# An attention block with gated experts on one core: own order for the last unit, V copied ahead, a wider low pass, another opening

## The chip, the cores and the metric

One core of a Trainium2 chip runs the whole computation. It has TensorE (PE; its weight loads are listed as PEld), VectorE (DVE), ScalarE (ACT), GpSimd (POOL) and SyncE (SP), which issues the DMAs. The metric is the device time in microseconds of one execution; lower is better.

## The reference

For x of 8 x 256 x 512 (2048 tokens), in float32:

```
xn = layernorm(x)
q, k, v = xn @ wq.T, xn @ wk.T, xn @ wv.T      # 32 query heads, 8 key/value heads, 128 wide
q, k = rotary(q), rotary(k)                    # q*cos + rotate_half(q)*sin
s = q @ k.T / sqrt(128), scaled for some keys, causal mask; p = softmax(s)
s_out = (p @ v) @ wo.T                         # each key head serves 4 query heads
gates = softmax over the top 2 of 4 router logits of xn
g = silu(sum_e gates_e * (xn @ A_e.T) @ B_e.T) # experts of rank 16
out = x + s_out * g
```

## The kernel before

**Precision.** Every large matmul runs in a reduced float form (fp32r), in three passes: each operand is split into a high part (a rounded copy, made by ACT) and a low part (the rest, made by DVE; for weights both parts by POOL), and hi*hi, hi*lo and lo*hi are added in PSUM (`three_pass`).

**Units.** The work is cut into 32 units: 8 key heads (groups) times 4 blocks of 512 tokens. A unit has four items: 2 sequences times 2 pairs of query heads. While unit u does its attention, PE also projects the keys, queries and V of later units. 16 tiles of 128 tokens gather the output in `y_sum`, one part for each of the 8 groups.

**One unit on PE** (`pe_unit`): for each item it transposes the probabilities (`turn_probs`, L565), computes the scores of the item two further on (`scores`, L554 to L558, into `pair`), multiplies probabilities with V (`prob_value`, L574, into `pv_ps`) and, between these, projects (`project`, L487, into `bank_a` or `bank_b`) or multiplies a tile with the output weights (`output_heads`, L581). Unit u finishes the last two output tiles of unit u-1. The transposes of item j wait for its scaled probabilities (`probs_ready`), the scores of item j+2 wait for both parts of item j's transposed probabilities (`pT_ready`), since they share a PSUM pair, and a product with V waits until the previous one has been taken from `pv_ps` (`attn_ready`).

**ACT and DVE** run lists in the same fixed order (`act_unit`, `dve_unit`). For an item: ACT copies the low scores (`low_scores`, L837), DVE masks and takes row extremes (`mask_rows`, L1215 to L1224), ACT takes exponents (L852), DVE inverts the sums (L1234), ACT scales (`normalise_rows`, L863), PE transposes, ACT makes the high part (`rows_high`, L871), DVE the low one (`rows_low`, L1204). The attention result is split by `attn_high` (L878) and `attn_low` (L1199). For a projected query head ACT swaps halves (`swap_halves`, L802 and L803), DVE multiplies by cos (L1169), POOL by sin (L391), DVE adds (L1178), ACT and DVE split (L810, L1184). V is copied by ACT (`copy_vT`, L824), transposed by PE (L544) and split. The next key projection into `bank_a` waits for the copy (`vT_done`).

**The experts** are side steps woven into units 0 to 7 (`side_plan`). The last of them, `d`, 16 times, multiplies the gated ranks `gm_T` (high part in partitions 0 to 63, low part in 64 to 127) first with `b_hi` on 128 partitions (L533), then the upper 64 partitions with `b_lo` (L534). The result becomes silu and goes to DRAM.

**The opening** is written out by hand (`pool_opening`, `act_opening`, `dve_opening`): statistics (L1047 to L1059), normalising shift of tiles (`x_shifted`, L945), transposes of x (`turn_x`, L494), their split (`x_high` L756, `x_low` L1073), the first weights (`first_high` L950, `first_low` L382). PE runs small matmuls (`keep_clock`, L705) until x is there.

**The end.** In the last group each tile gets its last part (`add_tile`, L1244), is multiplied with the gate (L1249) and gets x added by POOL (`add_residual`, L397). x and gate are loaded two tiles ahead by SP (`load_xg`). The last two tiles are computed in `pair[0]` after unit 31, each as two heads, then two more; DVE does all three operations on them (L1244, L1249, L1253) and SP stores them (`store_tile`).

Of the kernel before, what the change touches and what calls it, by code (L numbers as in the profile page):

```python
# [13 lines left out]
P = 128  # L14
# [47 lines left out]
def build(nc, x, w_seq, a_r, b_t, tables, out):  # L62
# [5 lines left out]
    with ctx:  # L68
# [36 lines left out]
        b_lo_full = sb("b_lo", [P, DM], F32R)  # L105
        b_lo = b_lo_full[0:ER, :]
# [54 lines left out]
        xg = [(mid_flat[:, 0:DM], mid_flat[:, DM:2 * DM]), (raw[:, 0, :], raw[:, 1, :]), (rot[:, 0, :], cosx[:, 0, :])]  # L161
# [66 lines left out]
        xg_in = [sem(f"xg_in{i}") for i in range(3)]  # L228
        y_gated = sem("y_gated")
        y_final = sem("y_final")  # L230
# [59 lines left out]
        def _(sp):  # L290
# [67 lines left out]
        def _(pool):  # L358
# [39 lines left out]

            def group(g, g_next):
# [3 lines left out]
                for i in range(first, BLOCKS):  # L403
# [38 lines left out]
                    if g_next is None:  # L442
                        add_residual(4 * i, 0)
                        if i < 3:
                            add_residual(4 * i + 1, 1)

            def pool_opening():
# [15 lines left out]
                sin_product(H2, 1)  # L463
                sin_product(H3, 1)
                sin_product(K, 2)
                inverse_std(3)
                sin_product(H0, 2)
                sin_product(H1, 2)
                split(0, WO)
                sin_product(H2, 2)  # L470
                split(0, WO + 1)
                split(0, WO + 2)
                sin_product(H3, 2)
                split(0, WO + 3)
# [7 lines left out]
            add_residual(TILES - 3, 1)  # L482
# [14 lines left out]
        def pe_side(u, j, p):  # L497
# [33 lines left out]
            else:  # L531
                t = i % BLOCK_TILES
                nc.tensor.matmul(o_ps[:, :], gm_T[:, t * P:(t + 1) * P], b_hi[:, :], start=True, stop=False)  # L533
                nc.tensor.matmul(o_ps[:, :], gm_T[0:ER, t * P:(t + 1) * P], b_lo, start=False, stop=True)\  # L534
# [163 lines left out]

        @block.tensor
        def _(pe):  # L700
# [44 lines left out]
            pe_unit(LAST)  # L745
            n = 4 * UNITS

            for t in range(2):
                output_heads(1, t, pair[0][:, t, :], range(0, 2))
            pe.wait_ge(attn_ready, n)  # L750
            for t in range(2):
                output_heads(1, t, pair[0][:, t, :], range(2, GROUP)).then_inc(o_done, 1)
# [128 lines left out]
        def act_unit(u):  # L881
# [70 lines left out]
        def act_opening():  # L952

            x_shifted(0, 1, 1)
            x_shifted(1, 2, 2)
            x_shifted(2, 3, 3)
            x_shifted(3, 4, 4)
            first_high(WK)
            first_high(WQ)
            x_high(0, first_banks[0])  # L960
            x_high(1, first_banks[1])
            x_high(2, first_banks[2])
            first_high(WQ + 1)
# [6 lines left out]
            x_shifted(4, 8, 5)  # L970
            q_high(H0, 1, None)
            swap_halves(H1, pv_ps, 1, H0, 1)
            swap_halves(H2, o_ps, 1, K, 1)
            x_high(4, first_banks[4])
            x_high(5, first_banks[5])
            k_high(1, None)
# [3 lines left out]
            q_high(H2, 1, None)  # L980
            q_high(H1, 1, None)
            swap_halves(H3, FIRST_H3, 1, H1, 1)
            first_low_scores()
            x_shifted(8, 12, 6)
            q_high(H3, 1, None)
            exponents(0, 1)
            v_high(1, None, pv_ps)
            normalise_rows(0, 1)
            swap_halves(H0, bank_b, 2, H3, 1)
# [12 lines left out]
            exponents(2, 3)  # L1002
            act_side(0, 1, 1)
            low_scores(3, 4)
            k_high(2, 4)
            q_high(H1, 2, 3)
            normalise_rows(2, 3)
            act_side(0, 1, 2)
            swap_halves(H2, bank_b, 2, K, 2)
            copy_vT(2, 1)  # L1010
            attn_high(1, 2, None)
            act_side(0, 1, 3)
            rows_high(2, 3, 2)
            exponents(3, 4)
            act_side(0, 2, 0)
            swap_halves(H3, bank_b, 2, H1, 2)
            act_side(0, 2, 1)
            attn_high(2, 3, None)
            low_scores(0, 5)
            normalise_rows(3, 4)  # L1020
            q_high(H2, 2, 4)
            swap_halves(K, bank_a, 3, H2, 2)
            q_high(H3, 2, 4)
            swap_halves(H0, bank_b, 3, H3, 2)
            rows_high(3, 4, 3)
            exponents(0, 5)
# [4 lines left out]
            exponents(1, 6)  # L1031

        @block.scalar
        def _(act):
            nc.scalar.dma_start(ident, tables[:, T_IDENT:T_COLS]).then_inc(ident_in, 16)

            act_opening()
            for u in range(1, WRITTEN):
                act_unit(u)
            loop(act, WRITTEN, LAST - 1, act_unit)  # L1040
            act_unit(LAST - 1)
            act_unit(LAST)
# [41 lines left out]
        def split_b():  # L1084
            nc.vector.wait_ge(bhi_done, 1)
            nc.vector.tensor_tensor(b_lo, b_raw[0:ER, :], b_hi[0:ER, :].bitcast(F32), ALU.subtract)\
                .then_inc(blo_done, 1)
# [148 lines left out]
        def add_tile(tile, done, start=False, final=None, bank=None, xg_set=None, tail=False):  # L1236
# [13 lines left out]
            if tail:  # L1250
                dve.wait_ge(y_gated, final + 1)
                dve.wait_ge(y_final, final)
                nc.vector.tensor_tensor(y, y, xg[xg_set][0], ALU.add).then_inc(y_final, 1)  # L1253
# [78 lines left out]
        def dve_opening():  # L1332

            first_statistics(0)
            first_statistics(1)
            first_statistics(2)
            shifts(0, 1, 1)
# [9 lines left out]
            block_statistics(2)  # L1347
            shifts(4, 8, 5)
            cos_product(K, bank_a, 1)
            cos_product(H0, bank_b, 1)  # L1350
            rotate(H0, 1)
            rotate(K, 1)
            q_low(H0, 1)
            cos_product(H1, pv_ps, 1, H0, 1)
            cos_product(H2, o_ps, 1)
            x_low(4, first_banks[4])
            x_low(5, first_banks[5])
            k_low(1)
            rotate(H2, 1)
            rotate(H1, 1)  # L1360
            x_low(6, first_banks[6])
            x_low(7, first_banks[7])
            q_low(H1, 1)
            q_low(H2, 1)
            shifts(8, 12, 6)
            cos_product(H3, FIRST_H3, 1, H1, 1)
            rotate(H3, 1)
            mask_rows(0, 1)
            q_low(H3, 1)
            row_inverse(1)  # L1370
            block_statistics(3)
            mask_rows(1, 2)
            rows_low(0, 1)
            v_low(1, pv_ps)
            cos_product(K, bank_a, 2, H2, 1)
            row_inverse(2)
            cos_product(H0, bank_b, 2, H3, 1)
            rotate(H0, 2)
            rotate(K, 2)
            attn_low(0, 1)  # L1380
            shifts(12, 16, 7)
            q_low(H0, 2)
            rows_low(1, 2)
            mask_rows(2, 3)
# [4 lines left out]
            dve_side(0, 1, 1)  # L1389
            mask_rows(3, 4)  # L1390
            k_low(2)
            q_low(H1, 2)
            dve_side(0, 1, 2)
            cos_product(H2, bank_b, 2)
            dve_side(0, 1, 3)
            attn_low(1, 2)
            rows_low(2, 3)
            rotate(H2, 2)
            dve_side(0, 2, 0)
            row_inverse(4)  # L1400
            cos_product(H3, bank_b, 2, H1, 2)
# [20 lines left out]
        def _(dve):  # L1422
# [4 lines left out]
            for u in range(FINAL, UNITS):  # L1427
                dve_unit(u)
# [44 lines left out]
```

## Time and profile before

| | before |
|---|---|
| runs, us | 1341.77, 1343.22, 1343.50; median 1343.22 |
| profiled execution, us | 1342.1 |
| its span, us | 1340.3 |
| PE busy | 1317.3 us, 98% |
| PE weight loads | 1106.4 us, 83% |
| DVE busy | 957.8 us, 71% |
| ACT busy | 971.7 us, 72% |
| POOL busy | 419.9 us, 31% |
| mean granted clock of PE | 0.994 |
| HBM over the span | 32 GB/s |

Busy shares are means over the whole span. A matmul's listed duration includes the filling and draining of the array and overlaps its neighbours: the distance between two starts says what it costs. The granted clock of a stretch is the mean of two levels, full (2.4 GHz) and half (1.2 GHz).

### The profile page before, as it was taken

What the parts mean: (1) busy time and instruction counts of PE and PEld (TensorE: products, weight loads), DVE (VectorE), ACT (ScalarE), POOL (GpSimd) and SP (SyncE); (2) the same over time, 40 slices, a digit from 0 to 9 for tenths busy, and PEclk for the clock granted to TensorE, in tenths of its full rate; (3) what the DMA queues carried; (4) which work ended last, traced back from release to release, by engine and by line L of the source; (5) the groups of instructions that cost most, each with busy time, mean ns of one, the idle gap of its engine ahead of it and who ended that gap; (6) DMA issues with size and microseconds to landing.
All of it is one profiled execution on the core that took longest, in us unless ns stands there. A gap on an engine that the chain in (4) does not pass through costs nothing.

```text
span 1340.3 us, 22644 instructions
## 1 busy us (share of the span) xinstructions
PE 1317.3 (98%) x7000; PEld 1106.4 (83%) x7000; DVE 957.8 (71%) x2440; ACT 971.7 (72%) x2529; POOL 419.9 (31%) x341
## 2 busy tenths in 40 slices
PE   8899999999999999999999999999999999999996
PEld 7788788878888888888888888888888888888885
DVE  6777587766767677777767677776777767767775
ACT  6977577776768777777777776877777777777673
POOL 5323322333114332223414133141422334133321
PEclk9899999999999999999999999999999999999998
DMA  6000000111001000000101000010100000002223
GB/s 220 9 25 20 25 9 20 53 42 47 31 17 32 16 23 8 16 16 16 31 0 31 0 17 30 0 31 0 31 16 3 29 16 23 8 32 86 84 79 113
DMA packets 23530, 43.66 MB, mean 33 GB/s; under 512 B 2496, under 2 KB 2752, under 8 KB 23488
## 3 DMA queue, kind: packets, MB, share of 16 engines
q1 hardware_dynamic: 20896, 38.74, 9.0%
q10 hardware_dynamic: 2592, 4.40, 0.9%
q8 instruction: 21, 0.34, 0.1%
q14 instruction: 21, 0.17, 0.0%
HBM read 34.74 MB, written 8.39 MB: 32 GB/s over the span
## 4 chain that ended last, share of the span: by engine, by line
PE 94%; ACT 2%; DVE 2%; issue 1%; DMA 0%; ACTq 0%
PE bank_a L487 19%; PE bank_b L487 19%; PE bank_b L581 13%; PE o_ps L581 13%; PE pv_ps L574 10%; PE pair L558 8%; PE pair L565 6%; PE pair L554 2%; PE pair L556 1%; PE o_ps L487 1%; PE bank_a L544 1%; ACT x_sb L945 1%; PE o_ps L534 1%; DVE pT_lo L1204 0%; PE pair L487 0%
## 5 line engine op out<-in xcount | busy, mean ns | idle before, releaser
L391 POOL TENSOR_TENSOR rot<-rot,tab 128x512 f32<-128x512 f32 x160 | 206.7, 1295 | 601.2 <-ACT rot L803 600.9
L871 ACT ACTIVATE pT_hi<-pair 128x768 fp32r<-128x768 f32 x128 | 103.9, 812 | 168.5 <-PE pair L565 167.7
L852 ACT ACTIVATE probs<-probs,row_min 128x128 f32<-128x128 f32 (+1 forms) x512 | 225.6, 447 | 0.1
L863 ACT ACTIVATE probs<-probs,row_inv 128x128 f32<-128x128 f32 (+1 forms) x512 | 190.7, 446 | 22.7 <-DVE row_inv L1234 22.3
L1204 DVE TENSOR_TENSOR pT_lo<-pair,pT_hi 128x768 fp32r<-128x768 f32 x128 | 121.6, 950 | 92.3 <-ACT pT_hi L871 92.0
L374 POOL TENSOR_TENSOR w_hi<-raw,zero 128x512 fp32r<-128x512 f32 x74 | 84.2, 1138 | 247.0 <-PE bank_a L487 131.0
L487 PE MATMUL bank_a<-xT_hi,w_hi 128*128 (+1 forms) x376 | 153.0, 407 | 0.7 <-DVE xT_lo L1073 0.6
L487 PE MATMUL bank_b<-xT_hi,w_hi 128*128 (+1 forms) x376 | 150.3, 400 | 0.0
L1184 DVE TENSOR_TENSOR q_lo<-cosx,q_hi 128x512 fp32r<-128x512 f32 x128 | 117.0, 915 | 44.3 <-ACT q_hi L810 44.1
L487 PE MATMUL bank_a<-xT_hi,w_lo 128*128 (+1 forms) x376 | 146.9, 391 | 0.0
L487 PE MATMUL bank_b<-xT_hi,w_lo 128*128 (+1 forms) x376 | 146.8, 391 | 0.0
L487 PE MATMUL bank_a<-xT_lo,w_hi 128*128 (+1 forms) x376 | 146.4, 389 | 0.0
L487 PE MATMUL bank_b<-xT_lo,w_hi 128*128 (+1 forms) x376 | 146.3, 389 | 0.0
L558 PE MATMUL pair<-k_parts,q_hi 128*128 128x256 f32 x512 | 116.7, 309 | 0.0
L565 PEld LDWEIGHTS pair<-tab,probs 128*128 128x128 f32 x768 | 91.7, 140 | 21.0 <-ACT probs L863 5.0
L565 PE MATMUL pair<-tab,probs 128*128 128x128 f32 x768 | 105.6, 274 | 3.0 <-ACT probs L863 3.0
L1215 DVE CUSTOM_DVE_ANT_0 probs<-pair,tab 128x256 f32<-128x256 f32 x256 | 106.4, 416 | 0.0
L581 PE MATMUL o_ps<-w_hi,attn_hi 128*128 128x512 f32 x252 | 104.7, 415 | 0.0
L581 PE MATMUL bank_b<-w_hi,attn_hi 128*128 128x512 f32 x252 | 101.4, 403 | 0.0
L377 POOL TENSOR_TENSOR w_lo<-raw,w_hi 128x512 fp32r<-128x512 f32 x74 | 99.0, 1338 | 5.8
L581 PE MATMUL o_ps<-w_hi,attn_lo 128*128 128x512 f32 x252 | 99.1, 393 | 0.0
L581 PE MATMUL bank_b<-w_hi,attn_lo 128*128 128x512 f32 x252 | 98.9, 393 | 0.0
(177 smaller groups left out, 3246.1 us busy)
## 6 DMA issues: line engine op xcount, KB each, us to landing
raw<-w_seq SPq DMA_DIRECT2D x76, 256.0 KB, 2.6
gate_scratch<-b_raw ACTq DMA_DIRECT2D x16, 256.0 KB, 2.0
out<-y_sum SPq DMA_DIRECT2D x16, 256.0 KB, 2.1
x_sb<-x SPq DMA_DIRECT2D x3, 1024.0 KB, 10.8
mid<-x SPq DMA_DIRECT2D x8, 256.0 KB, 2.7
mid<-gate_scratch SPq DMA_DIRECT2D x8, 256.0 KB, 2.9
raw<-x SPq DMA_DIRECT2D x7, 256.0 KB, 2.6
raw<-gate_scratch SPq DMA_DIRECT2D x7, 256.0 KB, 2.8
```

The costliest lines, as they stand in the source:

```text
L391: nc.gpsimd.tensor_tensor(v, v, tab[:, s:s + SEQ].unsqueeze(1).to_broadcast([P, 2, SEQ]), ALU.mult).then_inc(sin_done[kind], 1)
L487: mm = nc.tensor.matmul(dst, w(a, c), xs[:, c, bass.ds(x0, BLOCK)], start=(c == 0 and n == 0), stop=(c == DC - 1 and n == 2))
L558: mm = nc.tensor.matmul(ps[:, h, 2 * P:], a[:, head, late], k[:, k1], start=(n == 0), stop=(n == 2))
L565: mm = nc.tensor.transpose(ps[:, h, s * P:(s + 1) * P], probs[:, j % 2, h, s * P:(s + 1) * P], ident)
L574: mm = nc.tensor.matmul(dst, v[:, 2 * b + kb, :], p[:, :, c:c + (P if kb else SEQ)], start=(i == 0), stop=(i == 5))
L581: mm = nc.tensor.matmul(bank, a[:, h, rows], w[:, WO + h, :], start=(h == 0 and i == 0), stop=(h == GROUP - 1 and i == 2))
L852: a = nc.scalar.activation(s, s, ACT.Exp, bias=row_min[:, j % 2, i:i + 1], scale=-1.0, accum_out=row_sum[:, i:i + 1])
L863: a = nc.scalar.activation(s, s, ACT.Copy, scale=row_inv[:, i:i + 1])
L871: nc.scalar.activation(pT_hi[:, :, :], pair[j % 2][:, :, 0:ROWS], ACT.Copy).then_inc(pThi_done, 1)
L1184: nc.vector.tensor_tensor(q_lo[:, h, :], cosx[:, BUF[kind], :], q_hi[:, h, :].bitcast(F32), ALU.subtract)\
L1204: nc.vector.tensor_tensor(pT_lo[:, :, :], pair[j % 2][:, :, 0:ROWS], pT_hi[:, :, :].bitcast(F32), ALU.subtract).then_inc(pT_ready, 1)
L1215: return nc.vector.tensor_tensor_reduce(out=probs[:, par, h, s], in0=(probs[:, par, h, 0:P], pair[par][:, h, 2 * P:])[qt], in1=tab[:, T_MA ...
```

## The change

Six things are changed. (1) ACT copies V before it swaps the last query head, in every unit. (2) `b_lo` has 128 partitions, and the low pass of the experts uses all of `gm_T`. (3) The last unit has its own lists: `pe_closing`, `act_closing`, `dve_closing`; all four output tiles stand between its items. (4) Tiles 14 and 15 are multiplied with the gate and get x added by POOL (`open_tile`) before their last part is there; DVE multiplies that part with the gate and adds it (`close_tile`). (5) SP loads x and gate of tiles 15 and 14, the latter into `v_T` and `k_full`, before it stores tile 10. (6) The three opening lists have another order. The diff, cut to its core:

```diff
-        b_lo_full = sb("b_lo", [P, DM], F32R)
-        b_lo = b_lo_full[0:ER, :]
+        b_lo = sb("b_lo", [P, DM], F32R)
...
-        xg = [..., (rot[:, 0, :], cosx[:, 0, :])]
+        xg = [..., (rot[:, 0, :], cosx[:, 0, :]), (v_T[:, :], k_full[:, :])]
...
-            loop(sp, 0, TILES // 2 - 2, two_tiles)
+            loop(sp, 0, TILES // 2 - 3, two_tiles)
             sp.wait_ge(q_ready[H2], UNITS)
             load_xg(TILES - 1, 2)
-            store_tile(TILES - 4)
-            load_xg(TILES - 2, 0)
-            for t in range(TILES - 3, TILES):
+            sp.wait_ge(q_ready[K], UNITS)
+            sp.wait_ge(vt_ps, UNITS)
+            load_xg(TILES - 2, 3)
+            for s in range(2):
+                store_tile(TILES - 6 + s)
+                load_xg(TILES - 4 + s, s)
+            for t in range(TILES - 4, TILES):
                 store_tile(t)
...
+            def open_tile(t, s):
+                y = y_sum[:, t, :]
+                pool.wait_ge(xg_in[s], 32)
+                pool.wait_ge(y_added, 4 * UNITS - 2 * TILES + t + 1)
+                nc.gpsimd.tensor_tensor(y, y, xg[s][1], ALU.mult).then_inc(base_scaled, 1)
+                pool.wait_ge(base_scaled, t - TILES + 3)
+                nc.gpsimd.tensor_tensor(y, y, xg[s][0], ALU.add).then_inc(base_done, 1)
+            def pool_closing():
+                open_tile(TILES - 2, 3)
+                add_residual(TILES - 4, 0)
+                add_residual(TILES - 3, 1)
+                open_tile(TILES - 1, 2)
...
             def pool_opening():
+                first_low(WQ + 1)
                 first_low(WK)
                 first_low(WQ)
-                first_low(WQ + 1)
...
+                inverse_std(1)
                 sin_product(K, 1)
-                inverse_std(1)
+                split(0, WO)
                 sin_product(H0, 1)
-                inverse_std(2)
...
-                nc.tensor.matmul(o_ps[:, :], gm_T[0:ER, t * P:(t + 1) * P], b_lo, start=False, stop=True)
+                nc.tensor.matmul(o_ps[:, :], gm_T[:, t * P:(t + 1) * P], b_lo[:, :], start=False, stop=True)
...
+        def pe_closing():
+            pe.wait_ge(probs_ready, n - 3)
+            turn_probs(0)
+            output_tile(1, 0, n - 4, n - 7)
+            next_scores(2, n - 3, (), None)
+            pe.wait_ge(v_ready, UNITS)
+            prob_value(0)
+            pe.wait_ge(probs_ready, n - 2)
+            turn_probs(1)
+            output_tile(1, 1, n - 4, n - 6)
+            next_scores(3, n - 2, (), None)
+            pe.wait_ge(attn_ready, n - 3)
+            prob_value(1)
+            pe.wait_ge(probs_ready, n - 1)
+            turn_probs(2)
+            output_tile(0, 0, n - 2, n - 5, weights=KV_HEADS)
+            pe.wait_ge(pT_ready, n - 1)
+            prob_value(2)
+            pe.wait_ge(probs_ready, n)
+            turn_probs(3)
+            output_tile(0, 1, n - 2, n - 4)
+            pe.wait_ge(attn_ready, n - 1)
+            output_heads(1, 0, pair[0][:, 0, :], range(0, 2))
+            pe.wait_ge(pT_ready, n)
+            prob_value(3)
+            output_heads(1, 1, pair[0][:, 1, :], range(0, 2))
+            pe.wait_ge(attn_ready, n)
+            for t in range(2):
+                output_heads(1, t, pair[0][:, t, :], range(2, GROUP)).then_inc(o_done, 1)
...
             if not last:                                  # act_unit
+                copy_vT(c2, c1)
                 swap_halves(H3, bank_b, c2, H1, c2)
-                copy_vT(c2, c1)
                 low_scores(0, n4[5])
...
             x_shifted(0, 1, 1)                            # act_opening
+            x_high(0, first_banks[0])
             x_shifted(1, 2, 2)
+            first_high(WK)
+            first_high(WQ)
+            first_high(WQ + 1)
             x_shifted(2, 3, 3)
             x_shifted(3, 4, 4)
-            first_high(WK)
-            first_high(WQ)
-            x_high(0, first_banks[0])
             x_high(1, first_banks[1])
             x_high(2, first_banks[2])
-            first_high(WQ + 1)
             x_high(3, first_banks[3])
...
-            x_shifted(8, 12, 6)                           # between first_low_scores and exponents(0)
...
             rows_high(1, 2, 1)
-            x_shifted(12, 16, 7)
+            x_shifted(8, 12, 6)
...
+        def act_closing():
+            rows_high(0, 125, 124)
+            low_scores(2, 127)
+            normalise_rows(1, 126)
+            rows_high(1, 126, 125)
+            attn_high(0, 125, 122)
+            exponents(2, 127)
+            low_scores(3, 128)
+            normalise_rows(2, 127)
+            attn_high(1, 126, 122)
+            exponents(3, 128)
+            rows_high(2, 127, 126)
+            normalise_rows(3, 128)
+            rows_high(3, 128, 127)
+            attn_high(2, 127, 124)
+            attn_high(3, 128, 124)
...
             first_statistics(0)                           # dve_opening
+            shifts(0, 1, 1)
             first_statistics(1)
             first_statistics(2)
-            shifts(0, 1, 1)
...
             row_inverse(1)
-            block_statistics(3)                           # now behind cos_product(H0, bank_b, 1)
             mask_rows(1, 2)
             rows_low(0, 1)
...
+        def close_tile(t, done, s):
+            dve, i = nc.vector, t - TILES + 2
+            dve.wait_ge(base_done, i + 1)
+            dve.wait_ge(o_done, done)
+            nc.vector.tensor_tensor(xg[s][1], pair[0][:, i, :], xg[s][1], ALU.mult).then_inc(o_gated, 1)
+            dve.wait_ge(o_gated, i + 1)
+            dve.wait_ge(y_final, t)
+            nc.vector.tensor_tensor(y_sum[:, t, :], y_sum[:, t, :], xg[s][1], ALU.add).then_inc(y_final, 1)
+        def dve_closing():
+            rows_low(0, 125)
+            mask_rows(2, 127)
+            rows_low(1, 126)
+            add_tile(10, 123, final=10, bank=o_ps[:, :], xg_set=0)
+            attn_low(0, 125)
+            row_inverse(127)
+            mask_rows(3, 128)
+            attn_low(1, 126)
+            add_tile(11, 124, final=11, bank=bank_b[:, :], xg_set=1)
+            row_inverse(128)
+            rows_low(2, 127)
+            add_tile(12, 125, final=12, bank=o_ps[:, :], xg_set=0)
+            rows_low(3, 128)
+            attn_low(2, 127)
+            add_tile(13, 126, final=13, bank=bank_b[:, :], xg_set=1)
+            attn_low(3, 128)
+            close_tile(14, 127, 3)
+            close_tile(15, 128, 2)
```

The last unit before ran `pe_unit`, `act_unit` and `dve_unit` with `last` set, and the last 24 matmuls and the tail of DVE behind it.

## Rows read from the trace of the kernel before

**Rows 1.** PE timeline: start us, duration us, line, op, [idle us before, releaser].

```profile
14.03 0.50 PE L487 MATMUL bank_a<-xT_hi,w_hi 128*128 128x512 f32 x1 [0.61 <-DVE xT_lo L1073]
...
41.70 0.55 PE L565 MATMUL pair<-tab,probs 128*128 128x128 f32 x3 [0.87 <-ACT probs L863]
...
46.10 0.58 PE L554 MATMUL pair<-k_parts,q_hi 128*128 128x256 f32 x1 [3.52 <-DVE pT_lo L1204]
...
1311.62 0.39 PE L554 MATMUL pair<-k_parts,q_hi 128*128 128x256 f32 x1 [1.89 <-DVE pT_lo L1204]
...
1314.91 0.55 PE L565 MATMUL pair<-tab,probs 128*128 128x128 f32 x3 [0.79 <-ACT probs L863]
...
1318.36 0.98 PE L574 MATMUL pv_ps<-pT_hi,v_hi 128*128 128x512 f32 x2 [2.58 <-DVE attn_lo L1199]
```

**Rows 2.** Windows: stretch, length, busy us and counts by engine, PEclk, DMA share, GB/s.

```profile
40.00:50.00 10.00, 5.61 (x30) 4.87 (x28) 8.72 (x26) 8.32 (x24) 3.48 (x3) 0.70 0.00 0
1310.00:1320.00 10.00, 5.01 (x28) 4.13 (x28) 5.86 (x17) 8.97 (x29) 1.27 (x1) 0.86 0.41 145
1320.00:1330.00 10.00, 10.00 (x41) 8.28 (x40) 4.09 (x6) 2.12 (x4) 1.29 (x1) 0.80 0.06 23
```

**Rows 3.** Timeline of PE around the first and last late key projection.

```profile
417.15 0.49 PE L487 MATMUL bank_a<-xT_hi,w_hi 128*128 x1
...
1249.65 0.40 PE L574 MATMUL pv_ps<-pT_hi,v_lo 128*128 128x512 f32 x1
1250.00 0.50 PE L487 MATMUL bank_a<-xT_hi,w_hi 128*128 x1
1250.35 0.39 PE L487 MATMUL bank_a<-xT_lo,w_hi 128*128 x1
```

**Rows 4.** Timelines of ACT, DVE and PE in the unit of 1250 us.

```profile
1247.85 0.59 ACT L802 ACTIVATE rot<-bank_b 64x512 f32<-64x512 f32 x1 [0.18 <-PE bank_b L487]
...
1249.07 0.60 ACT L824 ACTIVATE v_T<-bank_a 128x512 f32<-128x512 f32 x1
...
1254.93 1.23 DVE L1184 TENSOR_TENSOR q_lo<-cosx,q_hi 128x512 fp32r<-128x512 f32 x1 [1.88 <-ACT q_hi L810]
...
1258.97 0.27 PE L554 MATMUL pair<-k_parts,q_hi 128*128 128x256 f32 x1
```

**Rows 5.** Timeline of PE around one of the 16 expert steps.

```profile
206.89 0.39 PE L533 MATMUL o_ps<-b_hi,gm_T 128*128 128x512 f32 x1
207.21 0.50 PE L534 MATMUL o_ps<-b_lo,gm_T 64*128 64x512 f32 x1
207.64 0.50 PE L487 MATMUL bank_b<-xT_hi,w_hi 128*128 128x512 f32 x1
207.97 0.39 PE L487 MATMUL bank_b<-xT_lo,w_hi 128*128 128x512 f32 x1
```

**Rows 6.** The page's part 5, two ACT groups: busy us, mean ns, idle before.

```profile
L852 ACT ACTIVATE probs<-probs,row_min 128x128 f32<-128x128 f32 (+1 forms) x512 | 225.6, 447 | 0.1
L863 ACT ACTIVATE probs<-probs,row_inv 128x128 f32<-128x128 f32 (+1 forms) x512 | 190.7, 446 | 22.7 <-DVE row_inv L1234 22.3
```

**Rows 7.** Chain that ended last, from 1309 us: start us, duration us, what.

```profile
1309.07 0.67 PE pair L565 x6
...
1321.90 3.82 PE o_ps L581 x12
...
1326.77 2.73 PE bank_b L581 x12
...
1333.62 0.70 DVE y_sum L1244
...
1337.13 0.69 DVE y_sum L1253
```

**Rows 8.** Timelines of PE weight loads and of ACT at the start.

```profile
7.70 0.50 PEld L494 LDWEIGHTS pair<-tab,x_sb 128*128 128x128 f32 x3 [0.35 <-ACT x_sb L945]
...
6.83 2.93 ACT L945 ACTIVATE x_sb<-x_sb,shift,rstd 128x512 f32<-128x512 f32 x4 [4.35 <-DVE shift L1059]
```

More of the change, by code:

```diff
@@ L226, in build @@
         y_added = sem("y_added")
-        xg_in = [sem(f"xg_in{i}") for i in range(3)]
+        xg_in = [sem(f"xg_in{i}") for i in range(4)]
         y_gated = sem("y_gated")
+        base_scaled = sem("base_scaled")
+        base_done = sem("base_done")
+        o_gated = sem("o_gated")
         y_final = sem("y_final")
@@ L533, in pe_side @@
                 nc.tensor.matmul(o_ps[:, :], gm_T[:, t * P:(t + 1) * P], b_hi[:, :], start=True, stop=False)
-                nc.tensor.matmul(o_ps[:, :], gm_T[0:ER, t * P:(t + 1) * P], b_lo, start=False, stop=True)\
+                nc.tensor.matmul(o_ps[:, :], gm_T[:, t * P:(t + 1) * P], b_lo[:, :], start=False, stop=True)\
                     .then_inc(side_ps, 1)
@@ L744, in _ @@
             pe_unit(LAST - 1)
[L745 to L752, printed above, removed]
+            pe_closing()
         def x_high(t, bank):
@@ L1234, in row_inverse, with add_tile @@
             nc.vector.reciprocal(row_inv[:, :], row_sum[:, :]).then_inc(inv_done, 1)
-        def add_tile(tile, done, start=False, final=None, bank=None, xg_set=None, tail=False):
+        def add_tile(tile, done, start=False, final=None, bank=None, xg_set=None):
             dve = nc.vector
@@ L1374, in dve_opening @@
             v_low(1, pv_ps)
+            row_inverse(2)
             cos_product(K, bank_a, 2, H2, 1)
-            row_inverse(2)
-            cos_product(H0, bank_b, 2, H3, 1)
-            rotate(H0, 2)
+            shifts(8, 12, 6)
+            shifts(12, 16, 7)
+            mask_rows(2, 3)
+            q_low(H0, 2)
+            rows_low(1, 2)
             rotate(K, 2)
             attn_low(0, 1)
[L1381 to L1384, printed above, removed]
             dve_side(0, 1, 0)
@@ L1389, in dve_opening @@
             dve_side(0, 1, 1)
+            dve_side(0, 1, 2)
             mask_rows(3, 4)
+            cos_product(H2, bank_b, 2)
+            q_low(H1, 2)
+            rows_low(2, 3)
+            dve_side(0, 1, 3)
             k_low(2)
[L1392 to L1395, printed above, removed]
             attn_low(1, 2)
-            rows_low(2, 3)
-            rotate(H2, 2)
+            cos_product(H3, bank_b, 2, H1, 2)
             dve_side(0, 2, 0)
             row_inverse(4)
-            cos_product(H3, bank_b, 2, H1, 2)
-            dve_side(0, 2, 1)
-            attn_low(2, 3)
+            rotate(H2, 2)
             rotate(H3, 2)
             mask_rows(0, 5)
+            attn_low(2, 3)
+            dve_side(0, 2, 1)
+            q_low(H2, 2)
             q_low(H3, 2)
-            q_low(H2, 2)
+            cos_product(H0, bank_b, 3, H3, 2)
             rows_low(3, 4)
-            cos_product(H0, bank_b, 3, H3, 2)
             cos_product(K, bank_a, 3, H2, 2)
+            add_tile(0, 1, start=True, bank=o_ps[:, :])
             row_inverse(5)
@@ L1414, in dve_opening @@
             attn_low(3, 4)
-            add_tile(0, 1, start=True, bank=o_ps[:, :])
+            add_tile(1, 2, start=True, bank=bank_b[:, :])
+            v_low(2)
             rotate(K, 3)
-            v_low(2)
             row_inverse(6)
-            add_tile(1, 2, start=True, bank=bank_b[:, :])
+        def close_tile(t, done, s):
[25 more added lines that the diff above has]
+            close_tile(15, 128, 2)
         @block.vector
@@ L1426, in _ @@
             loop(dve, WRITTEN, FINAL, dve_unit)
-            for u in range(FINAL, UNITS):
+            for u in range(FINAL, LAST):
                 dve_unit(u)
-            n = 4 * UNITS
-            for i in range(2):
-                t = TILES - 2 + i
-                add_tile(t, n - 1 + i, final=t, bank=pair[0][:, i, :], xg_set=2 * i, tail=True)
+            dve_closing()
 def kernel(**inputs):
```

89 lines of the change are left out of this document (45 added, 44 removed).

## The prediction

> **What bounds the kernel now.** I read the timeline of PE first, for idle time; then the windows, for its clock; then its starts one by one; the chain only for the end. PE's listed waits fall at the two ends of the run: 0.61 us at 14 us, 0.87 and 3.52 us at 42 to 46 us, 1.89, 0.79 and 2.58 us in the last unit [rows 1]. Both clusters also cost clock. The windows average a granted clock of 0.70, 0.86 and 0.80 [rows 2]; half speed is 1.2 GHz of 2.4, so the low time is 10 x (0.30, 0.14, 0.20) / 0.5 = 6.0, 2.8 and 4.0 us. PE had been mostly idle before each fall and busy again before each rise. Between the ends PE never stops, so what counts there is small holes between matmul starts. The regular step of a 512-column matmul is 2.73 / 12 = 0.227 us [rows 7]; a longer step is lost time that no list of waits shows. PE is the bound throughout; ACT and DVE count only where PE waits for them.
>
> **V copied ahead of the swap.** A key projection of the next unit overwrites bank_a and waits until ACT has copied V out of it. ACT swaps the last query head first (from 1247.85 us, after 0.18 us of idle), then copies V at 1249.07 to 1249.67 [rows 4]. PE's last probability-times-V matmul starts at 1249.65, the projection at 1250.00 and its second matmul at 1250.35 [rows 3]: 0.70 us for two steps that should take 0.45, so 0.24 us lost. This recurs in every unit from 417 to 1250 us, 22 times at a distance of (1250.00 - 417.15) / 21 = 39.7 us, each with the first matmul at 0.49 or 0.50 us. Copied first, V leaves ACT about 1.2 us earlier (two half swaps of 0.6), before PE asks: 22 x 0.24 = 5.3 us gone. In the last unit but one the later work of ACT starts 0.18 us sooner, which shortens a wait of PE there: 0.2 us. Sum 5.5 us. What is late in exchange is the swap, by at most 0.6 us; queued behind it are its sine product on POOL and the low part on DVE, which ends at 1254.93 + 1.23 = 1256.16, while PE needs it at 1258.97 [rows 4]. Those 2.8 us cover it, so the cost is nil. Bounds: 0 (the hole is something else's) and 5.8 us.
>
> **The low pass over 128 partitions.** The 16 expert steps multiply once with 128*128 weights and once with 64*128. The starts are 206.89, 207.21, 207.64, 207.97 [rows 5]: 1.08 us for three matmuls that should take 0.68, so 0.40 us lost, and the following projection's first matmul is part of it. After the change both passes have one form. 16 x 0.40 = 6.4 us. The column count is unchanged, and the split of b on DVE keeps 512 columns. Bounds: 0, if the hole belongs to the operands or the switch of bank, and 6.4 us. I take 6.4, since nothing else in the step differs from its neighbours and the loss sits on both sides of the 64-row matmul.
> The Trainium skill speaks both ways here. "TensorE: Matmul & The Clock Gate" (step-by-step part) says that the row count doesn't matter for the time; by that alone the edit would give 0. "TensorEngine Tiling (Array Packing)", key properties, says that a change of tiling mode drains the engine; by that the whole 6.4 goes. The trace, with the loss going in and coming out, sides with the second.
>
> **The last unit.** It keeps PE's work but spreads the four output tiles between the items, and interleaves ACT and DVE by hand. PE loses 1.89 + 0.79 + 2.58 = 5.3 us of idle now [rows 1], and runs 5.8 us (1318.36 to about 1324.2) at half clock, where it does half: 2.9 us; the twelve matmuls of one tile show it, 3.82 us against 2.73 [rows 7]. I walked the new order with the durations of the trace: six transposes 0.67, an output tile 2.73, scores or probability-times-V 1.05 (2304 columns at the step above), exponents of an item 225.6 / 128 = 1.8 us, its scaling 1.4 to 1.5 us [rows 6, 7], a 512-column operation on DVE 0.7, a mask about 2. Up to the end of item 0's product at 1306.2 nothing changes. Then:
> - item 1's scaling now stands behind the low copy of item 2's scores: it ends at 1307.0, PE waits 0.9;
> - scores of item 3 find their half ready; item 1's product waits 0.05 to 0.1 for the attention's low part, which stands behind tile 10 on DVE;
> - the transposes of item 2 wait for a scaling that ends at 1313.5: 0.8;
> - output tile (0,0) waits for the low part behind the fourth mask: 0.5; item 2's product 0.1;
> - item 3 finds everything, and the last twelve matmuls wait 0.25 for its low part.
> New idle 2.6 us, never over 0.9 at once, so I keep the full clock. PE ends 5.3 + 2.9 - 2.6 = 5.6 us earlier. The tail shortens too: from tile 14's last matmul to the end DVE now makes six operations, 1333.62 to 1337.82, 4.2 us [rows 7]; then x and the gate are already folded into tiles 14 and 15 by POOL (two operations each, in time by 1320 and 1327.6 in this walk), so that tile 15 follows 1.4 us behind tile 14 with two operations of 0.7: 2.9 us, 1.3 less. The added loads are the same four, two of them moved ahead of two stores on SP; the stores of tiles 10 and 11 wait for nothing of theirs. Sum 6.9, of which I take 6.8. Bounds: 3.9 (clock falls again) and 9.5 (no idle at all).
>
> **The opening.** Its new order makes ACT turn tile 0 before it shifts tile 1. But PE is in its warm-up matmuls until 7.70 - 0.35 = 7.35 us [rows 8], so the turn ends at 8.3 at best; ACT, which now runs without a gap from 6.83, would stand still from 6.4 to 8.4 and then still have three shifts of 0.7 [rows 8], three weight copies and three more tiles, 5.1 us and hand-over, before DVE's last low part of 0.7: first projection at 14.8 instead of 14.03 [rows 1]. On the other side the shift of tiles 8 to 11 (2.9 us) leaves the stretch before the exponents, and the last statistics leave the stretch before item 0's low part. Walking it, PE waits 0.6 for item 0's scores, 1.1 at the first transposes, 2.3 instead of 3.52 at 46 us, 1.2 at the next, and reaches the third transposes of unit 0 within 0.2 us of the old time. I take 0. The bounds are -3 (idle spread so that the clock stays, which frees the half of 5 us that run slow now) and +4 (the first projections catch the low clock, or POOL's weight split ahead of a sine product delays head 0 further).
>
> **Sum.** 5.5 + 6.4 + 6.8 + 0 = 18.7 us. The profiled execution took 1342.1 us (span 1340.3): 1323.4. The median of the runs is 1.1 above it: 1324.5 us, span about 1321.6.
>
> **Rivals.**
> - The 64-row matmul isn't what costs: 1324.5 + 6.4 = 1330.9. For it speaks that no row shows this step with 128 rows; against it, that the loss comes before the 64-row matmul as well as behind it [rows 5].
> - The V hole stays because the projection waits for something else of ACT or for the weight load: 1330. Against: the copy ends 0.33 us before the late start [rows 3, 4].
> - The ends go badly: low clock in the last unit (+2.9), or the opening's late start (+4, and with both 1331.4).
> - Slower: the swap that comes later makes PE wait for the last head. It decides once its low part is late by more than 2.8 us, where I count 0.6. If POOL let the sine product slip behind a pair of weight pieces in each unit, PE would stall some 1 us in 29 units: 1324.5 + 29 = 1353.5. Against it: PE sits 2.8 us clear.
> - The opening goes well, -3: 1321.5.
>
> **How the numbers follow.** Forecast 0.62, with its own range 1320.5 to 1328; 64 rows don't matter 0.11; V hole stays 0.04; ends go badly 0.13; opening well 0.06; slower 0.03, and 0.01 for a mix that ends at no change. The range for 8 in 10 takes the bounds of the unknown parts: 1319.5 to 1331.5. A change below 0.2%, 2.7 us, can't be told from none. All cases but the last two lie beyond it: faster 0.95, same 0.02, slower 0.03.
>
> **What would show it.** V: the step from the last probability-times-V matmul to the key projection is 0.23 us, unit distance 39.4 instead of 39.7. Experts: three steps of 0.23 around each pair. Last unit: no listed wait above 0.9 us, no low clock, and two DVE operations behind each of the last tiles. Opening: first projection at 14.8, wait at about 46 us down to 2.3. Wrong would be: any wait of PE for a query's low part in the middle; unit distance unchanged; the first projection past 16 us.

## The result and the profile after

| | before | after |
|---|---|---|
| median of 4 runs each, us | 1343.34 | 1326.65 (1326.10 to 1327.52) |
| profiled execution, its span, us | 1342.1, 1340.3 | 1326.8, 1324.6 |
| PE busy | 1317.3 us, 98% | 1303.3 us, 98% |
| ACT, DVE busy, us | 971.7, 957.8 | 972.5, 953.7 |
| mean granted clock | 0.994 | 0.999 |

The ratio is 0.9879, with an interval of 0.9866 to 0.9891: 16.7 us less, where 18.7 were forecast (1324.5 us). The forecast's range holds it. The two spans differ by 15.7 us, and where that comes from can be read off the starts of PE's scores, which stand in the same order in both traces (after minus before, us):

| at (before) | first scores 32.8 | 46.1 | 68.5 | 201.8 | 414.8 | 850.8 | 1259.0 | end |
|---|---|---|---|---|---|---|---|---|
| difference | +2.52 | +1.32 | +2.24 | +2.26 | -3.31 | -6.18 | -8.96 | -15.7 |

So the opening loses 2.3 us; the stretch from 202 to 415 us, with the expert steps, wins 5.6; the units up to the last one win 5.65 more at an even rate; the last one wins 6.7.

PE timeline of the kernel after, the idle rows (columns as in [rows 1]):

```profile
10.02 0.66 PE L517 MATMUL pair<-tab,x_sb 128*128 128x128 f32 x4 [0.53 <-ACT x_sb L1000]
...
12.28 0.66 PE L517 MATMUL pair<-tab,x_sb 128*128 128x128 f32 x4 [1.16 <-ACT x_sb L1000]
...
15.39 0.50 PE L510 MATMUL bank_a<-xT_hi,w_hi 128*128 128x512 f32 x1 [0.23 <-DVE xT_lo L1145]
...
35.29 0.36 PE L577 MATMUL pair<-k_parts,q_hi 128*128 128x256 f32 x1 [1.02 <-DVE q_lo L1255]
...
44.38 0.88 PE L588 MATMUL pair<-tab,probs 128*128 128x128 f32 x6 [1.03 <-ACT probs L918]
...
47.42 0.45 PE L577 MATMUL pair<-k_parts,q_hi 128*128 128x256 f32 x1 [2.16 <-DVE pT_lo L1275]
...
66.65 0.87 PE L588 MATMUL pair<-tab,probs 128*128 128x128 f32 x6 [0.76 <-ACT probs L918]
...
251.27 0.47 PE L556 MATMUL o_ps<-b_hi,gm_T 128*128 128x512 f32 x1 [0.35 <-DVE gm_T L1178]
...
1298.21 0.87 PE L588 MATMUL pair<-tab,probs 128*128 128x128 f32 x6 [0.79 <-ACT probs L918]
...
1304.87 0.88 PE L588 MATMUL pair<-tab,probs 128*128 128x128 f32 x6 [0.64 <-ACT probs L918]
...
1306.08 0.50 PE L604 MATMUL o_ps<-w_hi,attn_hi 128*128 128x512 f32 x1 [0.33 <-DVE attn_lo L1270]
```

The three waits of the last unit in [rows 1] (1.89, 0.79, 2.58 us) have become 0.79, 0.64 and 0.33. In the opening one long wait became many short ones, and the first projection starts at 15.39 instead of 14.03. The wait at 251.27 is new (it recurs at 293.52 and 335.80 with 0.36).

Windows of the kernel after (columns as in [rows 2]):

```profile
40.00:50.00 10.00, 6.80 (x37) 5.95 (x36) 6.36 (x20) 8.34 (x27) 4.87 (x5) 0.88 0.00 0
50.00:60.00 10.00, 8.92 (x51) 7.31 (x50) 7.57 (x20) 9.94 (x25) 4.38 (x5) 0.95 0.11 28
60.00:70.00 10.00, 9.24 (x48) 7.42 (x46) 6.46 (x19) 9.80 (x19) 3.77 (x3) 1.00 0.19 52
...
1310.00:1320.00 10.00, 9.95 (x49) 7.89 (x48) 4.88 (x7) 1.91 (x3) 6.79 (x5) 1.00 0.33 118
```

The last unit keeps the full clock. Near 50 us PE runs 10 x (0.12 + 0.05) / 0.5 = 3.4 us at half clock. ACT, in the fourth pair of numbers (behind PE, weight loads and DVE), is busy for 9.9 and 9.8 of 10 us there: in this stretch ACT is the bound, not PE.

PE timeline of the kernel after: an expert step, and the key projection of two units.

```profile
238.30 0.39 PE L556 MATMUL o_ps<-b_hi,gm_T 128*128 128x512 f32 x1
238.52 0.39 PE L557 MATMUL o_ps<-b_lo,gm_T 128*128 128x512 f32 x1
238.75 0.39 PE L510 MATMUL bank_a<-xT_hi,w_hi 128*128 128x512 f32 x1
238.98 0.39 PE L510 MATMUL bank_a<-xT_lo,w_hi 128*128 128x512 f32 x1
...
413.49 0.39 PE L597 MATMUL pv_ps<-pT_hi,v_lo 128*128 128x512 f32 x1
413.72 0.39 PE L510 MATMUL bank_a<-xT_hi,w_hi 128*128 x1
413.94 0.39 PE L510 MATMUL bank_a<-xT_lo,w_hi 128*128 x1
...
1241.15 0.39 PE L510 MATMUL bank_a<-xT_hi,w_hi 128*128 x1
```

All steps are 0.22 or 0.23 us, against 0.35 + 0.35 in [rows 3] and 0.32 + 0.43 + 0.33 in [rows 5]. The distance of two units is (1241.15 - 413.72) / 21 = 39.40 us (39.66 before).

The end of the chain that ended last, after (start us, duration us, what):

```profile
1317.58 1.67 PE pair L604 x6
...
1319.34 0.70 DVE k_full L1492
...
1320.07 0.59 DVE y_sum L1495
...
1320.70 0.70 DVE cosx L1492
...
1321.43 0.69 DVE y_sum L1495
```

Four DVE operations, from 1319.34 to 1322.12, are what is left behind tile 14's last matmul; six stood there before [rows 7].

### The profile page after: what moved, and what is told of

The parts are those of the page before. It is cut to its first block, busy times and chain, and to the rows that moved or that the text cites. A ratio compares the mean times of both kernels' runs of the same rounds, so it can differ in the third digit from the quotient of the medians.

```text
span 1324.6 us, 22633 instructions
## 1 busy us (share of the span) xinstructions
PE 1303.3 (98%) x7000; PEld 1106.3 (84%) x7000; DVE 953.7 (72%) x2438; ACT 972.5 (73%) x2529; POOL 427.0 (32%) x345
## 4 chain that ended last, share of the span: by engine, by line
PE 92%; ACT 3%; DVE 3%; issue 1%; DMA 0%; DVEq 0%; ACTq 0%
PE bank_b L510 19%; PE bank_a L510 18%; PE bank_b L604 13%; PE o_ps L604 12%; PE pv_ps L597 10%; PE pair L581 8%; PE pair L588 6%; PE pair L577 2%; PE pair L579 1%; PE o_ps L510 1%; PE bank_a L567 1%; ACT x_sb L1000 1%; ACT probs L918 0%; ACT probs L907 0%; ACT rot L857 0%
## 5 line engine op out<-in xcount | busy, mean ns | idle before, releaser
L510 PE MATMUL bank_a<-xT_hi,w_hi 128*128 (+1 forms) x376 | 149.9, 399 | 0.2 <-DVE xT_lo L1145 0.2
L1240 DVE TENSOR_TENSOR cosx<-bank_b,tab 128x512 f32<-128x512 f32 x94 | 64.7, 689 | 52.6 <-ACT rot L858 52.0
```

What stands on the lines that cost most here:

```text
L510: mm = nc.tensor.matmul(dst, w(a, c), xs[:, c, bass.ds(x0, BLOCK)], start=(c == 0 and n == 0), stop=(c == DC - 1 and n == 2))
```

## Experiments

Each kernel was timed in five rounds against the kernel before on the same chip.

| label | built on | median us | of before | ratio, interval |
|---|---|---|---|---|
| v_only | before | 1337.14 | 1342.41 | 0.9962, 0.9948 to 0.9976 |
| low_only | before | 1337.40 | 1342.41 | 0.9964, 0.9952 to 0.9976 |
| close_only | before | 1335.94 | 1342.41 | 0.9955, 0.9942 to 0.9969 |
| open_only | before | 1343.78 | 1342.41 | 1.0015, 1.0006 to 1.0024 |
| after_again | after | 1327.02 | 1341.92 | 0.9886, 0.9870 to 0.9903 |
| after_old_open | after | 1325.95 | 1341.92 | 0.9877, 0.9861 to 0.9894 |
| after_old_head | after | 1326.91 | 1341.92 | 0.9888, 0.9871 to 0.9904 |
| norm_first | after | 1326.01 | 1341.92 | 0.9880, 0.9863 to 0.9896 |
| low_96 | before | 1336.25 | 1343.39 | 0.9952, 0.9939 to 0.9966 |
| low_twice | before | 1347.22 | 1343.39 | 1.0030, 1.0018 to 1.0042 |
| v_later | before | 1350.18 | 1343.39 | 1.0052, 1.0038 to 1.0066 |
| best_try | after | 1325.29 | 1341.66 | 0.9874, 0.9858 to 0.9891 |

**v_only.**

```diff
-                swap_halves(H3, bank_b, c2, H1, c2)
                 copy_vT(c2, c1)
+                swap_halves(H3, bank_b, c2, H1, c2)
```

> The kernel before with one edit: V is copied ahead of the last query head's swap. If the hole in front of the key projection (0.12 us before it and 0.12 us behind its first matmul, 23 units) is what this edit takes away, the unit distance falls from 39.63 to 39.37 us and the time by 5.7 us, to 1337.6. Rival: the distance fell because of something else in the changed kernel (other alignment, other phase after the new opening); then this run stays within 1 us of 1343.3 and the hole is still there.

Measured: 5.3 us less. In its trace the starts gain 5.5 us between 68 and 1259 us. The opening, which this kernel doesn't change, came out 1.7 us later in the profiled execution, 1.09 us of it as a wait of PE. It begins with x, for which DVE waits 1.42 us, but the late x is not the whole of it: the small DVE operation at 21.21 us takes 1.19 us, where it took 0.17 in the kernel before. It started behind a product of POOL (21.09). In low_only and after_old_open it did so too, took 1.18 and 1.12 us, and PE waited the same 1.09. In the six other executions with the old opening it started before POOL's product, took 0.17 us, and PE had no such wait. In v_later, with x 0.17 us earlier than here, it was ahead by 0.14 us (21.05 against 21.19). The timelines of DVE and POOL in v_only, then PE's:

```profile
15.30 1.29 DVE L1047 BATCH_NORM_STATS2 stats<-x_sb 128x6 f32<-128x512 f32 x2 [1.42 <-DMA x_sb<-x]
...
21.21 1.19 DVE L1055 TENSOR_SCALAR meanvar<-meanvar 128x4 f32<-128x4 f32 x1
...
21.09 1.29 POOL L391 TENSOR_TENSOR rot<-rot,tab 128x512 f32<-128x512 f32 x1 [0.45 <-ACT rot L803]
```

```profile
29.85 1.26 PE L494 MATMUL pair<-tab,x_sb 128*128 128x128 f32 x8 [1.09 <-DVE xT_lo L1073]
...
419.07 0.39 PE L487 MATMUL bank_a<-xT_hi,w_hi 128*128 x1
419.30 0.39 PE L487 MATMUL bank_a<-xT_lo,w_hi 128*128 x1
```

The last two rows show the key projection without its hole. So the late copy of V caused it.

**v_later**, the counterpart: V is copied later still.

```diff
                 swap_halves(H3, bank_b, c2, H1, c2)
-                copy_vT(c2, c1)
                 low_scores(0, n4[5])
+                copy_vT(c2, c1)
```

> The kernel before with V copied still later, behind the low copy of the next scores (0.28 us of ACT). If the key projection waits for that copy, the hole of 0.24 us grows by the delay in the same 23 units: 23 x 0.28 = 6.4 us, 1348.8. Rival: the hole is a fixed cost of that place (a weight load that can't be taken ahead), and nothing changes.

Measured: 6.8 us more by the medians. PE's timeline, then ACT's copy:

```profile
417.94 0.40 PE L574 MATMUL pv_ps<-pT_hi,v_lo 128*128 128x512 f32 x1
418.57 0.49 PE L487 MATMUL bank_a<-xT_hi,w_hi 128*128 x1 [0.23 <-issue]
418.90 0.40 PE L487 MATMUL bank_a<-xT_lo,w_hi 128*128 x1
...
417.64 0.59 ACT L824 ACTIVATE v_T<-bank_a 128x512 f32<-128x512 f32 x1
```

The two steps take 0.96 us now, against 0.70 before and 0.45 unhindered. The copy stands one copy of low scores further back, and PE loses 0.26 us more per unit (7.0 - 1.1 over 21.5 units: 0.27). The scores' starts fall 1.1 us behind at 415 us and 7.0 at 1266. Of these recurring holes only the longer one is listed at all, and then as "issue", not as ACT. What ties both to the copy is its end: the projection starts 0.32 to 0.34 us behind it in this kernel (418.23 and 418.57) and in the kernel before (1249.67 and 1250.00) alike, in each of the 22 units.

**low_only.**

```diff
-        b_lo_full = sb("b_lo", [P, DM], F32R)
-        b_lo = b_lo_full[0:ER, :]
+        b_lo = sb("b_lo", [P, DM], F32R)
...
-  matmul(o_ps, gm_T[0:ER, t * P:(t + 1) * P], b_lo, ...)
+  matmul(o_ps, gm_T[:, t * P:(t + 1) * P], b_lo[:, :], ...)
```

> The kernel before with one edit: the low pass of the experts over 128 partitions. If the 64-row matmul costs 0.40 us at each of 16 steps, and 3 or 4 first steps of a block then show a wait for DVE instead (0.35 us each, as in the changed kernel), the time falls by 5.2 us to 1338.1. Rival: part of the 5.5 us that the two traces differ by between 185 and 400 us belongs to the V copy of these units; then about 4.5 us.

Measured: 5.0 us less by the medians; in the trace the expert units gain 5.65. From the matmul ahead of a step to the one behind it, 13 steps went from 1.31 or 1.19 us to 0.91 or 0.79 (0.40 each), the other three (the first `d` of a block) only from 1.43 to 1.13: 5.2 + 0.9 = 6.1 us at the steps themselves. 0.3 came back as a wait for V at 373.64. (The 64-row matmul of the kernel before reads partitions 0 to 63 of `gm_T`, the high part; over 128 the low part is multiplied with `b_lo` as well.)

**low_96.** As low_only, but the pass reads 96 partitions:

```diff
-  matmul(o_ps, gm_T[:, t * P:(t + 1) * P], b_lo[:, :], ...)
+  matmul(o_ps, gm_T[0:96, t * P:(t + 1) * P], b_lo[0:96, :], ...)
```

> The kernel before, with the low pass over 96 partitions in place of 64 (b_lo is filled on 128). If only the two array forms count, 64 rows and 128 rows, a 96-row matmul has the form of a 128-row one and the hole goes: as fast as the 128-row edit alone, 5 us under the kernel before. Rival: every row count other than the neighbours' costs a hole: then it stays at the time of the kernel before.

Measured: 7.1 us less by the medians, 5.5 at the expert units in the trace (the kernel before ran from 1341.2 to 1344.3 us in this series, so the trace says it better). PE's timeline:

```profile
206.88 0.39 PE L532 MATMUL o_ps<-b_hi,gm_T 128*128 128x512 f32 x1
207.10 0.40 PE L533 MATMUL o_ps<-b_lo,gm_T 96*128 96x512 f32 x1
207.34 0.40 PE L486 MATMUL bank_b<-xT_hi,w_hi 128*128 128x512 f32 x1
207.57 0.40 PE L486 MATMUL bank_b<-xT_lo,w_hi 128*128 128x512 f32 x1
```

Neither fewer rows than its neighbours nor the other operand makes the hole; the form with 64 rows does.

**low_twice.** The 64-row matmul is issued twice (its small term is added twice):

```diff
+  matmul(o_ps, gm_T[0:ER, t * P:(t + 1) * P], b_lo, start=False, stop=False)
   matmul(o_ps, gm_T[0:ER, t * P:(t + 1) * P], b_lo, start=False, stop=True)
```

> The kernel before with the 64-row matmul of each expert step issued twice, so that its small term is added twice. If the hole belongs to the change of form, each step costs one plain matmul more, 0.227 us: 16 x 0.227 = 3.6 us, 1346.0. Rival: each 64-row matmul is slow by itself (0.43 us as its step shows): 16 x 0.43 = 6.9 us, 1349.3.

Measured: 3.8 us more. PE's timeline:

```profile
207.11 0.39 PE L533 MATMUL o_ps<-b_hi,gm_T 128*128 128x512 f32 x1
207.43 0.49 PE L534 MATMUL o_ps<-b_lo,gm_T 64*128 64x512 f32 x1
207.77 0.39 PE L535 MATMUL o_ps<-b_lo,gm_T 64*128 64x512 f32 x1
208.09 0.50 PE L487 MATMUL bank_b<-xT_hi,w_hi 128*128 128x512 f32 x1
208.43 0.40 PE L487 MATMUL bank_b<-xT_lo,w_hi 128*128 128x512 f32 x1
```

Four steps take 1.32 us, 0.41 over 4 x 0.227. One 64-row matmul lost the same 0.40. So the price belongs to going in and coming out, and a second matmul of the form is free of it: 16 x 0.23 = 3.6 us is what was added.

**close_only.** The kernel before with `pe_closing`, `act_closing`, `dve_closing`, `open_tile`, `close_tile` and the new loads; V, `b_lo` and the opening as before:

```diff
+            pe_closing()      # and act_closing, dve_closing, pool_closing
```

> The changed kernel with V copy, low pass and opening put back: only the last unit's own order, with the two tiles folded ahead by POOL. If the two traces are read rightly the last unit alone gives 6.8 us: 1336.5. Rival: it needs the earlier V copy or another phase of the clock to avoid the half clock; then the clock falls here and it gives about 4 us, 1339.

Measured: 6.5 us less; the trace shows all of it (6.8) in the last unit. Its waits are the same three (0.80, 0.64, 0.33) and the clock stays at 1.00, so the last unit's gain doesn't hang on the other edits.

**open_only.** The kernel before with the three opening lists of the kernel after:

```diff
             x_shifted(0, 1, 1)
+            x_high(0, first_banks[0])
             x_shifted(1, 2, 2)
...
-            x_shifted(12, 16, 7)
+            x_shifted(8, 12, 6)
```

> The kernel before with the three opening lists of the changed kernel and nothing else. By the two traces every mark from 70 us on is 2.25 us later: 1345.6. Rival: the lag is bought back later (a wait at 204 us, or a clock that falls less) and the opening is worth nothing or a gain of 1 to 2 us: 1341.5 to 1343.3.

Measured: 1.4 us more by the medians, 0.8 to 3.2 by the ratio; +1.4 in the trace at the scores of 1259 us, +1.0 at its end. The opening costs, if less than the 2.25 us expected.

**after_old_open.** The kernel after with the three old opening lists (the reverse of the diff above).

> The changed kernel with the three opening lists of the kernel before. If the new opening costs what its own run showed (1.4 us by medians, 1.4 to 2.3 by the marks), this is faster than the changed kernel by 1.4 to 2.3 us: about 1324.8 when that one has 1326.6. Rival: the old opening loses the same elsewhere in an execution (in two of three traces it waited 1.1 us more at 29.9 us), and the two are equal within 0.7 us.

Measured: 0.7 us under the kernel after's first median and 1.1 under its second; its starts stand 0.8 to 1.0 us ahead from 70 us to the end, although that execution had the 1.09 us wait of v_only. The gain lies between the 1.4 to 2.3 us expected and the rival's 0.7. PE's idle rows:

```profile
14.16 0.50 PE L510 MATMUL bank_a<-xT_hi,w_hi 128*128 128x512 f32 x1 [1.68 <-DVE xT_lo L1145]
...
30.05 1.25 PE L517 MATMUL pair<-tab,x_sb 128*128 128x128 f32 x8 [1.09 <-DVE xT_lo L1145]
...
43.27 0.87 PE L588 MATMUL pair<-tab,probs 128*128 128x128 f32 x6 [0.87 <-ACT probs L918]
...
47.67 0.58 PE L577 MATMUL pair<-k_parts,q_hi 128*128 128x256 f32 x1 [3.53 <-DVE pT_lo L1275]
```

The old 3.5 us wait is back, yet the next stretch is faster: from the scores at 47.67 to those at 69.89 us PE needs 22.2 us, the kernel after 23.3 (47.42 to 70.69), both with 3.4 us at half clock. One shift of x less lies in it.

**after_old_head.** Only the head of the lists is put back; ACT's part is shown, and one line each of POOL's and DVE's lists goes with it:

```diff
             x_shifted(0, 1, 1)
-            x_high(0, first_banks[0])
             x_shifted(1, 2, 2)
-            first_high(WK)
-            first_high(WQ)
-            first_high(WQ + 1)
             x_shifted(2, 3, 3)
             x_shifted(3, 4, 4)
+            first_high(WK)
+            first_high(WQ)
+            x_high(0, first_banks[0])
```

> The changed kernel with only the head of its opening put back (all four tiles shifted before the first is turned; up to the first projection), the rest of the new opening kept. If the loss of the opening is its late first projection (15.39 against 14.03 us), this gains 1.2 to 1.4 us and its first projection starts at 14.0. Rival: the new order behind 50 us is bound by ACT, which holds both late shifts there; then the early gain is eaten by waits at 44, 47 and 66 us, and it stays within 0.5 us of the changed kernel.

Measured: no difference by the medians (1326.91 against 1327.02); in the trace the first projection starts at 14.05, 1.34 us earlier, of which 0.41 goes to a wait for x at 29.73 and 0.7 to 0.8 stays. That is half of the 1.5 us that open_only is behind at 68 us and a third of the kernel after's 2.24, by single executions; the timing can't confirm so little: the medians show what the rival said, less than 0.5 us.

**after_again.** The kernel after, unchanged, as the yardstick of its series.

> The changed kernel once more, as the yardstick for the other runs of this call: 1326.6, within 0.7 us.

Measured: 1327.02 us. Its profiled execution reached the first scores 1.35 us later than the first one did. The granted clock was 0.83 in the window of 10 to 20 us, where it was 1.00 in the other, and the first projection started at 16.37 us, past the 16 us that the prediction had named as a sign of being wrong. One kernel's opening thus differs by over a microsecond between executions.

**norm_first.** In `act_closing` item 1's scaling goes ahead of item 2's low scores:

```diff
             rows_high(0, 125, 124)
-            low_scores(2, 127)
             normalise_rows(1, 126)
+            low_scores(2, 127)
```

> The changed kernel with one edit in its last unit: ACT scales item 1's probabilities before it copies item 2's low scores. The wait of 0.79 us in front of the second transposes (at 1298 us) was worked out from this order beforehand. If it is real and on the path, it goes, and the time falls by 0.5 to 0.8 us. Rival: the masks of item 2 get their input later and the time moves to the wait of 0.64 us before the third transposes; then no change.

Measured: 1.0 us under after_again. The 0.79 us wait is gone, the other two stay, and PE's last transposes but one start 0.88 us earlier, in an execution whose opening was 0.15 later:

```profile
1303.99 0.87 PE L588 MATMUL pair<-tab,probs 128*128 128x128 f32 x6 [0.61 <-ACT probs L918]
1305.20 0.50 PE L604 MATMUL o_ps<-w_hi,attn_hi 128*128 128x512 f32 x1 [0.34 <-DVE attn_lo L1270]
```

**best_try.** after_old_open and norm_first together.

> The changed kernel with the opening of the kernel before and with item 1 scaled before item 2's low copy in the last unit. Singly these measured 1.1 and 1.0 us under the changed kernel of the same call (1327.0), each with runs that overlap it little. If they add, the ratio to the kernel before is 0.9870, some 2.1 us under the changed kernel. Rival: the waits they remove are partly each other's noise, and this lies with the two singles at a ratio of 0.9877.

Measured: 1325.29 us, the lowest median of all, 1.4 and 1.7 us under the two medians of the kernel after. The intervals of the ratios overlap, so it rests on the traces that both parts give a microsecond. The ratio lies midway between the 0.9870 expected and the rival's 0.9877. Its own opening ran 6.8 us at half clock (0.81 and 0.85 in the windows from 40 to 60 us) where that of after_old_open ran 3.4.

## Why the prediction was right, step by step

**V: right.** 5.5 us forecast; 5.3 by v_only's median, 5.65 over the units in the changed kernel, with the step of 0.23 and the distance of 39.4 as named. The swap that comes later made nobody wait: no wait for a query's low part appears in the middle. The 0.2 us in the last unit but one didn't come: the wait there is 0.16 us shorter (1.16 for 1.32), and 0.1 is lost behind it. v_only and v_later, which move the copy alone, leave nothing of the rival in which the hole stays for another reason.

**The low pass: mechanism right, size 1.2 to 1.4 us off.** All of the 0.40 us goes at 13 steps. At the three others the first matmul waits for the low part of `gm_T`, which DVE makes behind a mask; the old hole hid it. In the changed kernel PE arrives yet earlier, for V's holes are gone too (in v_only, which has the old low pass, such a wait shows as 0.16 us at 295.78 and 0.15 at 339.51). The wait is 0.35 us, and such a step takes 1.51 us, 0.08 more than before. So 13 x 0.40 - 3 x 0.08 = 5.0 us at the steps, and 5.2 by the starts of the scores (5.57 less one V hole, 0.37 us at 377 us). The reason given for the 6.4, "nothing else in the step differs from its neighbours", held for PE but asked nothing about who delivers the operand next. The rival "64 rows don't matter" is dead (low_96 and low_twice). The rule on tiling modes that the prediction took from the Trainium skill, "TensorEngine Tiling (Array Packing)", key properties, agrees with the rows: the 64-row matmul costs 0.40 us in and out together. What the prediction took from the Trainium skill, "TensorE: Matmul & The Clock Gate", step-by-step part, on the row count is said there of the weight load. Read as a rule for the whole step it held for the 96 rows of low_96 (0.23 us) and failed for these 64.

**The last unit: right.** 6.8 forecast, 6.8 measured in close_only (6.7 in the changed kernel), and of the waits named (0.9, 0.8, 0.5 and 0.25 for the last low part) the first three came at 0.79, 0.64 and 0.33. The clock held, as it did in close_only, so its rival fell. The tail is four operations, 2.8 us (2.9 forecast).

**The opening: the step that failed.** It was taken as 0. It costs 1.4 us by open_only's median, 0.7 to 1.1 by after_old_open's, and 2.3 between the two traces. The wait at 46 us was forecast well (2.3, came 2.16), and those at the first scores and transposes roughly (0.6 and 1.1; 1.02 and 1.03); the 1.2 "at the next" came as 0.20 at 51.66. Two things were missed. First, the head: forecast at 14.8, it was 15.39 in the changed kernel and 14.85 in open_only, so its size depends on the execution. Second, the end of the walk, "reaches the third transposes of unit 0 within 0.2 us of the old time". They start at 66.65, 1.96 us later than before (64.69). ACT is the bound from 50 to 67 us, and both remaining shifts of x now lie in it. ACT's timeline of the kernel after:

```profile
53.27 2.92 ACT L1000 ACTIVATE x_sb<-x_sb,shift,rstd 128x512 f32<-128x512 f32 x4
...
60.44 2.94 ACT L1000 ACTIVATE x_sb<-x_sb,shift,rstd 128x512 f32<-128x512 f32 x4
...
65.10 1.49 ACT L918 ACTIVATE probs<-probs,row_inv 128x128 f32<-128x128 f32 x4
```

The scaling at 65.10 ends behind them and gives the 0.76 us wait at 66.65, which the prediction's walk didn't have. That the order at 53 and 60 us causes it is read from the traces (the wait is in all five with the new order there, 0.74 to 0.76, and in none of the nine with the old one); no kernel moved that one shift alone.

**The sum.** By the traces: 5.65 + 5.57 + 6.8 - 2.26 = 15.8 us of the 15.7. The singles' medians add to 5.3 + 5.0 + 6.5 - 1.4 = 15.4, the whole gives 16.7 (14.9 in the second series). The difference is inside what the openings of single executions scatter. Of the forecast 18.7 the medians gave 16.7 and the traces 15.7; by the traces the low pass gave 1.2 less and the opening 2.3 less than forecast, V 0.5 more (5.65 and the 0.37). The own range, up to 1328 us, held the result with 1.3 us to spare.

**The shorter stretch at half clock in the opening** (3.4 us for 7.0). All five profiled executions with the new order behind 40 us had 3.4. Of the nine with the old one seven had 6.8 or 7.0, and two, low_96 and after_old_open, had 3.4 as well. So it goes with the new order but doesn't need it: after_old_open and best_try ran the same opening lists with 3.4 and 6.8. What decides between the two is open. The rival of -3 us for a clock that stays didn't come.

**Smaller slips in the rows.** PE doesn't quite run without a stop between the ends: waits of 0.89 us at 57.82 and 0.67 at 201.82 stand in the trace before, and both are still there after. The chances of the cases called faster add to 0.96, not 0.95.

## What to carry to other kernels

In an engine that never idles, compare the distance of starts with the regular step: two of the three gains here, 22 holes of 0.24 us and 16 of 0.40, stood in no list of waits. When a hole goes, ask which operand it was hiding; and when work is moved out of one wait, follow it until the engine that carries it has slack again, not until the next wait. An opening that differs by over a microsecond between executions of one kernel needs a kernel of its own and several executions to be priced.

## What was not expected of the hardware

- A 96-row matmul between 128-row ones costs a plain step (0.23 us), a 64-row one 0.40 us more, and a second 64-row one beside it 0.23 again.
- A DVE operation of 128x4 elements took 1.12 to 1.19 us in the three executions with the old opening in which it started just behind a POOL product, and 0.17 in the six in which it started before it. Between v_later and v_only 0.17 us in the landing of x turned the order round, and PE then waited 1.09 us.
- Behind a late start the second matmul is late too (0.35 us for 0.23), which makes half of the hole of [rows 3]; the late start itself stands 0.33 us behind the end of the copy that it waited for. Nothing of that hole is listed; of v_later's step of 0.63 us, 0.40 too long, 0.23 is.
- The first four transposes of x took 0.66 us in close_only and after_old_open and 1.12 in best_try, which has the same opening lists, at a granted clock of 1.00 each.
